# Second batch's projections moved into the opening of an attention kernel, and its row normalisation moved to ScalarE

## The reference, cut to what matters

```python
def xattn(q, k, v, mask, w_q, w_k, w_v, w_o):        # x: (4, 512, 256), ctx: (4, 1024, 256)
    query, key, value = (split_heads(t @ w.T) for t, w in ((q, w_q), (k, w_k), (v, w_v)))
    query, key = rope(query), rope(key)
    scores = einsum('bhqd,bhkd->bhqk', query, key) / 4
    scores = where(mask[:, None, None, :] == 0, -10000.0, scores)
    x = einsum('bhqk,bhkd->bhqd', softmax(scores), value)
    return merge_heads(x) @ w_o.T
x = x + xattn(layernorm(x), ctx, ctx, mask, w_q, w_k, w_v, w_o)
x = x + ffn_block(layernorm(x))       # small causal attention, router, top 2 of 8 experts
```

## Time and profile before

| | us |
|---|---|
| median of 3 runs (795.46 to 797.01) | 795.62 |
| the profiled execution | 792.0 |
| its span | 790.2 |
| PE busy in it | 698.4 (88%) |
| DVE busy in it | 562.5 (71%) |
| ACT busy in it | 488.0 (62%) |
| POOL busy in it | 355.1 (45%) |
| mean granted TensorE clock | 0.935 |

### The profile page before, as it was taken

One profiled execution on the slowest core, in us unless ns is written; L12 is line 12 of the kernel. 1 busy time (PEld: TensorE's weight loads), 2 busy tenths in 40 slices (PEclk: granted clock), 3 DMA queues, 4 the chain that ended last, 5 costly groups with the idle time before them and its releaser, 6 DMA issues. The chain is left out here.

```text
span 790.2 us, 13501 instructions
## 1 busy us (share of the span) xinstructions
PE 698.4 (88%) x4402; PEld 428.4 (54%) x4402; DVE 562.5 (71%) x930; ACT 488.0 (62%) x968; POOL 355.1 (45%) x262
## 2 busy tenths in 40 slices
PE   3256689999999998999999999988978889999996
PEld 2252334444344443444433443476767779999995
DVE  4958778778788778788798984367997426555653
ACT  2010348777677776777778777856746047667673
POOL 4966425118604139345938880000045713544444
PEclk9775769999899999999999999999989799999999
DMA  9576246766667664326877870059736546623321
GB/s 256 187 235 183 104 150 190 229 160 204 213 207 243 174 187 160 115 83 197 292 250 244 274 265 6 1 156 409 249 67 179 223 109 143 117 31 40 39 28 20
DMA packets 59719, 130.73 MB, mean 165 GB/s; under 512 B 8868, under 2 KB 26308, under 8 KB 58196
## 3 DMA queue, kind: packets, MB, share of 16 engines
q1 hardware_dynamic: 33364, 72.86, 28.4%
q0 software_dynamic: 16848, 35.95, 17.8%
q10 hardware_dynamic: 9440, 21.06, 9.0%
HBM read 80.80 MB, written 69.39 MB: 190 GB/s over the span
## 5 line engine op out<-in xcount | busy, mean ns | idle before, releaser
L749 DVE TENSOR_REDUCE mx<-wide 128x2 f32<-128x1024 f32 x256 | 307.5, 1223 | 76.4 <-PE wide L903 74.9
L609 ACT ACTIVATE probs<-narrow 128x512 f32<-128x512 f32 x492 | 265.5, 599 | 87.7 <-PE narrow L942 86.6
L903 PE MATMUL wide<-kst,qst 49*128 49x512 f32 x512 | 181.1, 481 | 22.2 <-DVE mx L749 12.6
L942 PE MATMUL narrow<-qst,kst 51*128 51x512 f32 x492 | 188.8, 458 | 1.9 <-ACT probs L609 1.5
L942 PEld LDWEIGHTS narrow<-qst,kst 51*128 51x128 f32 x492 | 80.7, 189 | 135.8 <-issue 57.9
L957 PE MATMUL values<-probs,vaug 128*17 128x512 f32 x1024 | 139.0, 616 | 1.4 <-ACT probs L609 0.8
L1707 POOL DMA_INDIRECT out<-res,token x39 | 60.8, 1558 | 91.4 <-DMA out<-res,token 60.3
L903 PEld LDWEIGHTS wide<-kst,qst 49*128 49x128 f32 x512 | 74.7, 199 | 36.6 <-DVE mx L749 23.1
L454 POOL TENSOR_TENSOR turn_b<-turn_a,tab 128x1024 f32<-128x1024 f32 x10 | 24.1, 2410 | 69.8 <-ACT turn_a L603 69.2
L1239 POOL DMA_DIRECT2D out<-xt x4 | 5.5, 1376 | 108.5 <-DVE xt L1434 108.5
L1732 ACT ACTIVATE h_hi<-narrow 128x512 fp32r<-128x512 f32 x39 | 23.3, 598 | 41.3 <-PE narrow L1812 41.3
(11 more groups left out here) (287 smaller groups left out, 1370.1 us busy)
## 6 DMA issues: line engine op xcount, KB each, us to landing
list_rows<-in_w ACTq DMA_DIRECT2D x56, 342.0 KB, 4.7
kst<-k_pieces SPq DMA_DIRECT2D x14, 784.0 KB
k_pieces<-turn_a SPq DMA_DIRECT2D x16, 512.0 KB, 4.6
w_hi<-w_hi SPq DMA_DIRECT2D x16, 512.0 KB, 10.8
w_lo<-w_lo SPq DMA_DIRECT2D x16, 512.0 KB, 11.6
turn_a<-in_w POOLq DMA_DIRECT2D x11, 512.0 KB, 5.6
w_hi<-turn_b POOLq DMA_DIRECT2D x11, 512.0 KB, 3.0
w_lo<-turn_a POOLq DMA_DIRECT2D x11, 512.0 KB, 4.7
```

The lines of the kernel that those rows point to most:

```text
L609: nc.scalar.activation(probs[:, n % NP, :], score_bank(n), ACT.Exp, scale=DK ** -0.5).then_inc(exp_done, 1)
L749: last = nc.vector.tensor_reduce(mx[quad % 2][:, qt, :, hp, kh], slot[:, :, :], axis=AX.X, op=ALU.max)
L903: last = nc.tensor.matmul(slot[:, i, :], qst[u % 3][r:r + R_MAX, h, P * qt:P * qt + P], kst[u % 3][r:r + R_MAX, h, 512 * kh:512 * kh + 512 ...
L942: nc.tensor.matmul(score_bank(n), kst[u % 3][r:r + R_ALL, h, P * kt:P * kt + P], qst[u % 3][r:r + R_ALL, h, :], start=True, stop=True).the ...
```

## The change: what it does

The opening gets more jobs. After `c 1 1` come the four rows tiles of `xn` for batch 1, its `xT`, and the four values halves of the first context half. The 16 maxima of quad 0 follow; from the tenth on, each is followed by one half: the four halves of `k 1 1`, then values halves (six halves behind maxima ten to fifteen, two behind the sixteenth). Each of the four maxima of quad 1 is followed by a half of the queries of batch 1. So what was in periods 0 to 7 and 13 to 20 for batch 1 is gone from them.

`xn` of batches 1 to 3 is done by ACT as `Identity` with a scale and a bias for each partition (four instructions, in four different periods), from a new small tile `shift`; that of batch 0 stays on DVE.

The freed periods take the next jobs earlier (by period, before and after): `c 2` 16 and 20, now 3 and 12; `k 2` 21 to 28, now 9 to 19; `xn 2` at the end of 28, now one tile in each of 18 to 21; `xT 2` 32, now 24; `q 2` 35 to 39, now 26 to 30; `v 2` 45 to 52, now 36 to 44; `oP 0` 40 to 44, now 45 to 48; `c 3` 48 and 52, now 39 and 48; `k 3` 53 to 60, now 50 to 59; `xn 3` end of 60, now 58 to 61. From period 62 on the lists agree.

On SP, `load_context(1, 1)` goes ahead of the last keys of quad 0, `store_turned(1, 0)` ahead of the first max rows, and in the loop the second context load and the store of the first key block go ahead of one `load_max_rows` (the store ahead of two loads too).

```diff
+PLAN = [(18, (26, 27, 28, 30), (), (3, 12), (9, 10, 11, 14, 16, 17, 18, 19), ()),
+        (None, (), (4, 5, 6, 7, 9, 10, 11, 12), (7, 16), (18, 19, 20, 22, 23, 24, 25, 27), (13, 14, 15, 16)),
+        (-6, (3, 4, 6, 7), (13, 14, 15, 16, 17, 18, 19, 20), (), (), (8, 10, 11, 12)),
+        (None, (), (), (), (), (8, 10, 11, 12))]
...
-    before += [("rate", 1), ("c", 1, 0), ("k", 1, 0, 0), ("k", 1, 0, 1), ("rope", 1, 0), ("c", 1, 1)] + maxes(0)
-    before += [*maxes(1)[:2], ("k", 1, 1, 0), *maxes(1)[2:AHEAD], ("k", 1, 1, 1), ("rope", 1, 1)]
+    before += [("rate", 1), ("c", 1, 0), ("k", 1, 0, 0), ("k", 1, 0, 1), ("rope", 1, 0), ("c", 1, 1)]
+    before += [("xn", 1, n) for n in range(QT)] + [("xT", 1)] + [("v", 1, 0, n // 2, n % 2) for n in range(4)]
+    halves = [("k", 1, 1, n // 2, n % 2) for n in range(4)] + [("v", 1, 1, n // 2, n % 2) for n in range(4)]
+    first = maxes(0)
+    for n, j in enumerate(first):
+        before += [j] + (halves[n - 9:n - 8] if 9 <= n < 15 else halves[6:] if n == 15 else [])
+    before += [("rope", 1, 1)]
+    for n in range(AHEAD):
+        before += [maxes(1)[n], ("q", 1, n // 2, n % 2)]
+    before += [("rope", 1, 2)]
...
         load_keys(0, slice(0, 2), (0,))
+        load_context(1, 1)
         load_keys(0, slice(2, PAIRS))
-        load_context(1, 1)
         load_queries(1)
         load_keys(1)
         load_keep(1, 1)
+        store_turned(1, 0)
         load_max_rows(0)
-        store_turned(1, 0)
         store_turned(1, 1)
...
+            if t + 1 < B:
+                load_context(t + 1, 1)
             load_max_rows(4 * b + 2)
             if t < B:
                 load_queries(2 * t)
+            load_max_rows(4 * b + 3)
             if t + 1 < B:
-                load_context(t + 1, 1)
-            load_max_rows(4 * b + 3)
+                store_turned(t + 1, 0)
             if t < B:
                 load_queries(2 * t + 1)
                 load_keys(2 * t + 1)
                 load_max_rows(4 * b + 4)
             if t + 1 < B:
-                store_turned(t + 1, 0)
                 store_turned(t + 1, 1)
...
+            if kind == "xn":
+                b, t = j[1:]
+                if t == 0:
+                    act.wait_ge(*by_pe(("xT", b - 1)))
+                    act.wait_ge(shift_set, 1)
+                n = QT * b + t
+                nc.scalar.activation(xn[:, t, :], xt[:, n, :], ACT.Identity, scale=rstd[:, n:n + 1], bias=shift[:, n:n + 1]).then_inc(act_done, 1)
+                return
...
+            if i > 0:
+                nc.vector.scalar_tensor_tensor(out=shift[:, tiles], in0=mv[:, tiles, 0], scalar=-1.0, in1=rstd[:, tiles], op0=ALU.mult, op1=ALU.mult).then_inc(shift_set, 1)
```

More of the change, by code:

```diff
@@ L59, in attention_order @@
         g, t = 32 * b, b + 1
[L60 to L66, removed]
+        x, q, v, c, k, o = PLAN[b]
+        if x is not None:
+            r = 2 if b == 0 else t
+            timed += [(g + x + n, ("xn", r, n)) for n in range(QT)] + [(g + x + 6.2, ("xT", r))]
+            timed += [(g + at + 0.2, ("q", r, n // 2, n % 2)) for n, at in enumerate(q)] + [(g + q[-1] + 0.5, ("rope", r, 2))]
+        timed += [(g + at + 0.2, ("v", t, n // 4, n // 2 % 2, n % 2)) for n, at in enumerate(v)]
+        if k:
+            timed += [(g + at + 0.5, ("c", t + 1, n)) for n, at in enumerate(c)]
+            timed += [(g + at + 0.2, ("k", t + 1, n // 4, n // 2 % 2, n % 2)) for n, at in enumerate(k)] + [(g + k[4 * n + 3] + 0.5, ("rope", t + 1, n)) for n in range(2)]
         if b > 0:
-            timed += [(g + 2.2, ("oT", b - 1))] + [(g + x, ("oP", b - 1, n // 2, n % 2)) for n, x in enumerate((8, 10, 11, 12))]
+            timed += [(g + 2.2, ("oT", b - 1))] + [(g + at + 0.2, ("oP", b - 1, n // 2, n % 2)) for n, at in enumerate(o)]
     for quad in range(QUADS - 1):
@@ L95, in attention_order @@
     for b in range(1, B):
-        assert index[("xT", b - 1)] < index[("xn", b)] and index[final(order, "q", b - 1)] < index[("xT", b)]
+        assert index[("xT", b - 1)] < index[("xn", b, 0)] and index[final(order, "q", b - 1)] < index[("xT", b)]
         assert all(index[final(order, "v", b - 1, g)] < index[("c", b, g)] for g in range(2))
@@ L127, in cross_attention @@
     rstd = sb("rstd", [P, NT])
+    shift = sb("shift", [P, NT])
     xT_hi = sb("xT_hi", [P, KC, SQ], F32R)
@@ L171, in cross_attention @@
     values_prepared, filled = sem("values_prepared"), sem("filled")
-    var_set, std_set = sem("var_set"), sem("std_set")
+    var_set, std_set, shift_set = sem("var_set"), sem("std_set"), sem("shift_set")
     dve_step, pool_step = sem("dve_step"), sem("pool_step")
@@ L185, in on_act @@
     def on_act(j):
-        return j[0] in ("w", "xT", "v", "mxt", "oT", "oT0", "oT1", "root0") or (j[0] in ("q", "k") and not turned_by_dve(j))
+        return j[0] in ("w", "xT", "v", "mxt", "oT", "oT0", "oT1", "root0") or j[0] == "xn" and j[1] > 0 or (j[0] in ("q", "k") and not turned_by_dve(j))
     def lo_by_pool(j):
@@ L191, in on_dve @@
     def on_dve(j):
-        return j[0] in ("xn", "xT", "max", "nm", "out", "oT", "oT0", "oT1", "oP", "oP1", "moments", "tile0", "again0", "rates0") or j in (("c", 0, 0), ("c", 0, 1)) or j in BY_DVE or (j[0] in ("q", "k") and turned_by_dve(j)) or (j[0] == "w" and not lo_by_pool(j))
+        return j[0] in ("xT", "max", "nm", "out", "oT", "oT0", "oT1", "oP", "oP1", "moments", "tile0", "again0", "rates0") or j in (("xn", 0),) or j in (("c", 0, 0), ("c", 0, 1)) or j in BY_DVE or (j[0] in ("q", "k") and turned_by_dve(j)) or (j[0] == "w" and not lo_by_pool(j))
     def on_pool(j):
@@ L696, in _ @@
             if kind == "xn":
-                b = j[1]
-                if b > 0:
-                    dve.wait_ge(*by_pe(("xT", b - 1)))
                 for t in range(QT):
-                    last = nc.vector.tensor_scalar(xn[:, t, :], xt[:, QT * b + t, :], mv[:, QT * b + t, 0:1],
-                                                   rstd[:, QT * b + t:QT * b + t + 1], ALU.subtract, ALU.mult)
+                    last = nc.vector.tensor_scalar(xn[:, t, :], xt[:, t, :], mv[:, t, 0:1], rstd[:, t:t + 1], ALU.subtract, ALU.mult)
             elif kind == "moments":
@@ L886, in job @@
             if kind == "xT":
-                pe.wait_ge(*by_dve(("xn", j[1])))
+                pe.wait_ge(*(by_act(("xn", j[1], QT - 1)) if j[1] > 0 else by_dve(("xn", 0))))
                 for k in range(KC):
```

## The result

The changed kernel has a median of 792.36 us in 6 runs (789.2 to 794.24), the kernel before 796.89 in 6 runs beside it (795.46 to 798.03): ratio 0.994, interval 0.9912 to 0.9967. It is 4.5 us faster, not 27, and the forecast of 768.6 with its range from 764 to 778 was wrong. A second set gave 788.64 against 796.11, ratio 0.9882 (0.9848 to 0.9915).

The account below looks back on a forecast made before the run. PE was taken to pace attention periods, except in the opening, first periods and ends of the first two batches. 12.3 + 7.3 + 8.0 - 0.6 = 27.0 us less gave a 768.6 us median; range 764 to 778.

Parts of the forecast that it names:

- Other queues: SP's waits moved ahead of max rows: both cost 0, with some 5 us in hand in the tighter one.
- the term for batch 1: Batch 1: query halves and `xT 2` gone, end stall 13.26 to 8.40, `xn 3` on ACT added; 8.0 us less.
- Rival 4: SP's waits for POOL's rotation blocks and `c 2 0` delay max rows from period 16; 796 or more, chance 0.03.
- The opening: Start to first score: 0.6 us longer in all, bounds -1 and +11; first score 0.3 later than 88.68.
- The start: Opening before the maxima: normalisations end at 55.1, PE's halves by 58.5 to 62; cost 0 to 0.8, taken as 0.3.
- The slow rounds: Opening, halves between maxima: 0.9 us per round at 1.2 GHz, two or three rounds until the clock rises at about 77.
- rival 1: Clock stays low in the opening: opening costs 7.8 us, first periods perhaps 2, total 777.8; chance 0.10.
- First periods and batch 0: First four distances 23.47 to 11.2, 12.3 us less; rest of batch 0, 27 periods, 7.3 us less.
- `xn` on ACT: Normalisations of later batches on ACT: 0.52 us each, no table load; 0.15 each taken as cost, bounds 0 and 4.2.
- Rival 2: ACT becomes late: eight normalisations delay exponentials, 3.6 us plus 2 for the clock, total 774.2; chance 0.13.
- Behind period 62: Attention periods from 62 on: the job lists agree, so everything shifts as a block; difference 0.
- Second block: From the last values group to the end of the span: difference 0.

Follow-up runs that it names:

- run 2: Changed kernel, with the fourth batch's first key block stored after the loads and max rows, as before the change: 786.68 us, ratio 0.9756 to the kernel before.
- run 1: Changed kernel, with queries and keys of a batch's second half loaded before the wait and store of the first key block: 801.35 us, ratio 0.9913.
- runs 5 and 6: The kernel before and the changed kernel, both unedited, profiled again on one chip: 795.67 us and 788.64 us.
- the held run: run 2's kernel, with POOL's block `rope 1 1` held until DVE has finished `nm 0`: 778.57 us, ratio 0.9804.
- runs 4 and 7: 4: run 1's kernel, batch 1 query halves ahead of `mxt 0`, 804.24 us, ratio 0.9952. 7: run 2's kernel, eight maxima's products made twice, 776.87 us, ratio 0.9741.
- run 11: the held run's kernel, with four values halves of batch 1's second context half moved from the opening to periods 1 to 4: 780.67 us, ratio 0.979.
- Run 8: run 2's kernel, with `xn` of batches 1 to 3 back on DVE, one tile in each of four periods: 786.35 us, ratio 0.9851.
- runs 5 to 12: Eight executions on one chip: both kernels unedited, and edited versions of the changed kernel; medians from 776.87 to 795.67 us.
- runs 1 to 4: Four executions on another chip: three edits of the changed kernel, and the kernel before with only `xn` moved to ACT; 786.68 to 804.24 us.

## Why the prediction was wrong, step by step

**Other queues, and with it the term for batch 1: the failed step.** It said of the store of `k 3 0` that "the rows behind it are made in period 61, seven periods or 20 us later", at cost 0. The wait did end 7 us ahead of the rows. What was not asked is what SP sends in those 7 us: the stores and the loads behind the wait are released all together, 6.5 and 14.8 us of transfers, and the small one that PE needs queues behind them. That is the cost that the working put at 0. It is 10.7 us in this trace (13.31 for 2.66, of which 10.4 is waiting) and 1.1 in the next distance, at the lower clock; run 2, which takes it away, shows it, and run 1 makes the same from the other side. The other 0.5 of batch 1's 11.2 stays in run 2 too (103.7 for a forecast of 103.1). One distance of batch 1 is longer in both (4.07 for 3.08), with a cast of `mh` of 1.42 us beside POOL in it (see the opening). That it is the cast that costs this is seen at the same place of batch 0: the changed kernel has 1.40 for the cast and 4.07 for the distance there, run 2 has 0.18 and 3.09. Rival 4 had the right place, waits moved ahead of max rows, but the wrong link: it looked at the second context load, priced lateness alone and gave 0.03.

**The opening: 0.3 later was forecast for the first score, it came 4.8 later (93.52 against 88.68), and in five other executions with its opening (one with the rows on DVE) 1.2 to 6.5 later than that 88.68.** In runs 5 and 6, on one chip, it was 7.4 (94.08 against 86.70). The start was right: normalisation ended at 54.4, PE's block at 60, the maxima began at 60.48 and `c 1 1` was split at 71.3, 0.43 behind PE's need. The slow rounds came as said in the changed kernel: clock up near 75, `nm` at 82.34 where the maxima were to end at 82.5. In other executions they did not: in run 1 PE was busy 16.0 of 16.0 us from 72 to 88 at 0.50, the clock rose near 90, all six rounds took 2.30 us against 1.33, and `nm` came at 87.30. That was rival 1, at 0.10 too rarely: of nine executions with these rounds four have `nm` at 86.5 to 87.3 and five at 81.3 to 83.3. And what the working did not contain at all: behind `nm` the cast of 16 elements, 0.17 before, took 1.85 beside POOL's block, which the change starts 9.5 us earlier; PE idled 2.12 us, its clock fell to 0.50, and three of the four query rounds took 2.3. I had named no work of POOL's beside DVE's small step. Of the two, the cast is shown by the held run and the ends beside POOL's; that mending it makes the whole faster is not, and what decides when the clock rises stays open: runs 4 and 7 were made for it and missed.

**First periods and batch 0: right**, -11.8 and -7.2 for -12.3 and -7.3. But the first four distances are 11.6 to 12.9 in eight executions with the changed opening or an edit of it, and 17 in three (runs 4, 7, 11), in which the clock was at 0.50 for most of them; run 11 has four values halves in them besides. So -11.8 is one of two outcomes, and luck has a part in it.

**`xn` on ACT: right in place and price.** All twelve took 587 to 603 ns (four in 2.06 us, back to back, in the opening); there is no table load before any of them, and no distance was lengthened by more than was allowed. Run 8 shows that the place mattered: 0.7 to 1.1% of the time. Rival 2 (ACT becomes the late one) did not come. On DVE alone a tile is in fact shorter (0.41), and the longer one on ACT is cheaper here, where POOL and the maxima stand beside DVE's.

**Behind period 62** the lists agree, but not the time: 3.1 us more here, 2.7 in runs 5 and 6. A third is the first distance after the stall (4.76 for 3.71), which belongs to the failed step. The rest is `mxt` periods in which the cast again meets POOL, now splitting weights (casts of 2.06, 0.89 and 1.30 us): single distances of 4.33, 3.54 and 3.37 for 3.08. The kernel before has such too in its second profile (4.34, 4.05), so this goes by how the engines happen to meet.

**Second block:** 0 was forecast; 1.6 on one chip, within what its executions differ by there (2.9).

Put together, with the store last the forecast would have been off by 6 to 10 us instead of 22: 1 to 6 in the opening, up to 5 in the first periods, and one or two behind. That split is read from single executions and isn't separated by timed runs.

## What to carry to other kernels

When a wait is moved in a queue of DMAs, ask not only whether it ends in time, but what it lets go when it ends, and whether something small and urgent is issued right behind. The bulk's own time can be read off the trace ahead of the change: here 15 us of loads, released 7 us before the rows. Put bulk either long before or behind what is urgent, and ask of each transfer who waits for it. A block of work that is moved to overlap another engine's small step on the critical path may cost that step ten times its length and then PE's clock. Normalisation may be the shorter instruction on VectorE (0.41 us alone against 0.60) and still belong on ScalarE, when VectorE's stop is what stops PE. And run the parts of a change one by one: here the small part, the rows on ACT, brought most of it.

## What the runs showed of the hardware that was not expected

- A cast of 128x16 elements on DVE took 0.17 us with POOL idle and up to 2.32 beside a POOL instruction of 2.4 us on SBUF, and ended 0.02 to 0.04 us after it; a reduce of 128x32 elements beside the same instruction took 0.19 (82.34), and maxima read from PSUM kept their 1.2 us. Beside POOL's instruction on `keep`, run 2's cast took 0.17 as well.
- The query and key loads of a half batch, 2.4 MB in packets of 8 and 16 KB, took 14.6 to 15.9 us from first packet to last at period 63 in five executions (some 160 GB/s); the 1.6 MB of stores ahead of them in the changed kernel went in packets of 2 KB in 6.5 us (240 GB/s).
- PE at 1.2 GHz stayed there through 16 us in which it was busy without a gap (run 1), with matmuls of 49 rows and of 128 rows in turn; in the changed kernel, with the same instructions, it had risen by 75, soon after the rounds began at 71.4.
- The second block took 282 and 287 us in the first two profiles and 284 to 287 in the eight of one chip (runs 5 to 12), and 295 to 297 on another (runs 1 to 4), whatever the kernel; so whole spans of different chips are not compared here.
